# A fused Perceiver layer: the weight product Wq Wk' formed ahead of x, two banks for cross-attention scores, self-attention scores in pairs

## Chip, cores, metric

The kernel is one program on one NeuronCore of a Trainium2 chip. The metric is device time in microseconds (us) of one execution. All numbers here are of the kernel before unless said otherwise.

## What is computed

```python
# x: (4, 128, 512), ctx: (4, 2048, 384), all float32
q, k, v = ln(x) @ Wq + bq, ctx @ Wk + bk, ctx @ Wv + bv
x = x + softmax(q @ k.T / sqrt(512)) @ v             # one head, 2048 keys per batch
cq, ckv = ln(h @ W_dq) * g + b, ln(h @ W_dkv) * g + b # h = ln(x)
K, V = split(ckv @ W_ukv)                            # 16 heads of 32
s = (cq @ W_uq) @ K.T / sqrt(32)                     # zeros and future keys masked
x = x + (softmax(s) @ V) @ W_o.T
# then 16 routed experts (top 4 of 2 groups of 4) and a shared one, relu(x W)^2 W'
```

## The kernel before

**Cross-attention without keys or values.** The scores are q·k = (ln(x) Wq + bq) Wk'·ctx, plus a constant of each query, q·bk. So the kernel forms `qk = Wk q` once for all 512 tokens (`qk_h`, `qk_l`) and multiplies it with the transposed context. Nearly every product is done in three matmuls (`split_mm`): each operand is kept as a rounded part (`_h`, cast by ScalarE) and the rest (`_l`, subtracted by VectorE or GpSimd).

**Setup, before the steps.** SyncE's queue loads x, `wq` (1 MB in one transfer), small vectors, context chunks and `wkT`. VectorE takes moments and normalises four batches (`moments`, `normalise`), PE transposes them (`rows_T`, L1234), ScalarE and VectorE make `xT_h` and `xT_l` (L645, L859). PE forms qT (48 matmuls of 512 columns into banks 4 to 7), ScalarE and VectorE evict it with the bias (L687, L1024), PE forms qk (36 matmuls into banks 4 to 6), it is evicted (L690, L1028), and 32 matmuls of two columns give q·bk (L1262, L1263, `c_mm`), reduced to `ccol`.

**Steps.** After that each engine runs the same loop over steps 1 to 33, and in a step each does its share of several stages in an order written out by hand. There are 16 chunks g of 512 keys, four a batch. In step g+1 PE computes the scores of chunk g into bank 2 (9 matmuls, L1227 to L1229), VectorE evicts them with their maximum (L1078); ScalarE and VectorE split the next chunk into `cT_h`, `cT_l` (L652, L1012), with two buffers of `cT`. Softmax needs the maximum over four chunks, so five steps later (`LAG`) PE transposes the weights (L1360) and multiplies them with the untransposed context (L1436; a float32 matmul is two passes in the trace). Each step after that carries a piece of a batch's remaining work: steps 9, 13, 17 and 21 project with Wv and add the result, steps 12, 16, 20 and 24 make `qk_s` and `v_s` (L1404, L1472).

**Self-attention units.** From step 13 on one unit u enters a step: four heads that sit in rows 32r to 32r+31 of `qk_s`. `unit_scores` (L1334) are four matmuls of contraction 32 into bank 6 or 0, VectorE masks and takes the maximum (L867, L869, L871), ScalarE exponentiates (L759), GpSimd divides (L570), two steps later PE transposes (L1344). Before, most units from 6 on are issued at the end of the step ahead of their own (`early`); a unit waits for the exponentials of unit u-2.

**Queues.** SyncE's queue issues in program order and stops at each wait. The transposed chunks (`load_chunk_T`, four slots) wait until VectorE has split the chunk four before; the others (`load_chunk`, three slots) wait for L1436 of the chunk three before. The first three of these are loaded in setup. `woT` is loaded ahead of transposed chunk 4, behind a wait for the low part of `wv`.

**Later stages** (from about 235 us) are the experts; the change touches there only which semaphore a weight load counts on.

## Time and profile before

| | |
|---|---|
| median of 3 runs | 414.12 us (413.81 to 414.54) |
| the profiled execution's own time | 414.46 us |
| its span | 412.7 us |
| PE busy | 368.5 us |
| DVE (VectorE) busy | 252.6 us |
| ACT (ScalarE) busy | 166.0 us |
| POOL (GpSimd) busy | 97.5 us |

The span runs from the first to the last instruction of the profile; the time is 1.76 us longer. PE's busy time counts pipelined matmuls up to their modelled ends, so starts are safer to read than durations. PEclk is the granted clock of PE in tenths, or as a mean in a window.

### The profile page before, as it was taken

Reading aid. Unit: us, or ns where it says so; the run is one execution under the profiler, and the core shown is the slowest. Engines: PE = TensorE matmul, PEld = TensorE weight load, DVE = VectorE, ACT = ScalarE, POOL = GpSimd, SP = SyncE. Lnnn points to the kernel's source line nnn. Section 1 sums busy time; section 2 is a strip of 40 time slices with the busy share of each in tenths; the row PEclk is TensorE's granted clock in tenths of the full one; section 3 lists DMA queues with packets and bytes.
Section 4 is the critical chain, followed back from the end, with each engine's and each line's share of the span. In section 5 each row is a group of like instructions: output and inputs, shape, how many; then the busy total and the mean of one; then the engine's idle time right before and its main releaser. Section 6 shows DMA issues by size and latency. Waiting matters only on the chain.

```text
span 412.7 us, 5990 instructions
## 1 busy us (share of the span) xinstructions
PE 368.5 (89%) x2116; PEld 254.5 (62%) x2116; DVE 252.6 (61%) x474; ACT 166.0 (40%) x398; POOL 97.5 (24%) x111
## 2 busy tenths in 40 slices
PE   1799869999999998997898799995999999999994
PEld 1578547677677766776677588882544554554452
DVE  5782765565487475477845658933113677776677
ACT  2624455535555564454747606200232332332310
POOL 4740000000011111312413140025334444441200
PEclk9999689999999999999979899996999999999998
DMA  7990396885322254070000460579963433331393
GB/s 246 417 381 5 138 353 261 294 276 197 113 76 78 86 182 169 25 305 2 26 2 28 152 231 22 181 294 360 422 230 122 128 116 116 127 123 59 119 370 124
DMA packets 15998, 71.74 MB, mean 174 GB/s; under 512 B 2913, under 2 KB 2913, under 8 KB 13281
## 3 DMA queue, kind: packets, MB, share of 16 engines
q1 hardware_dynamic: 11808, 57.72, 37.7%
q0 software_dynamic: 4160, 13.63, 9.6%
q8 instruction: 17, 0.28, 0.3%
q14 instruction: 13, 0.10, 0.1%
HBM read 62.96 MB, written 8.39 MB: 173 GB/s over the span
## 4 chain that ended last, share of the span: by engine, by line
PE 64%; DVE 15%; DMA 7%; ACT 4%; issue 4%; POOL 3%; SPq 1%; DVEq 0%; POOLq 0%; ACTq 0%
PE bank L1580 10%; PE bank L1436 9%; PE bank L1554 8%; PE bank L1227 7%; PE bank L1229 6%; PE bank L1228 6%; DMA xs<-x_rows,from_row 4%; DVE cT L1012 4%; PE bank L1334 3%; DVE res L1207 3%; PE bank L1535 2%; DMA raw<-in_wkT 2%; PE bank L1565 2%; PE bank L1404 2%; DMA ring_T<-in_ctxT 2%
## 5 line engine op out<-in xcount | busy, mean ns | idle before, releaser
L1436 PE MATMUL bank<-ring,wT 128*128 128x384 f32 x128 | 43.9, 486 | 0.0
L1012 DVE TENSOR_TENSOR cT<-ring_T,cT 128x512 fp32r<-128x512 f32 x48 | 37.9, 839 | 8.5 <-ACT cT L652 8.4
L1147 DVE COPY xsT<-bank 128x512 f32<-128x512 f32 x24 | 16.6, 690 | 35.1 <-PE bank L1535 25.2
L592 POOL DMA_INDIRECT xs<-x_rows,from_row x24 | 23.3, 969 | 52.1 <-DVE to_row L993 29.8
L547 POOL TENSOR_TENSOR rstd<-var,mhalf 128x1 f32<-128x1 f32 x12 | 6.9, 578 | 111.9 <-DVE var L844 111.9
L1436 PEld LDWEIGHTS bank<-ring,wT 128*128 128x128 f32 x128 | 23.9, 191 | 13.5
L599 POOL DMA_INDIRECT y_rows<-ys,to_row x21 | 22.4, 1067 | 41.2 <-ACT ys L804 41.2
L652 ACT CAST cT<-ring_T 128x512 fp32r<-128x512 f32 x48 | 26.8, 617 | 12.9 <-PE bank L1229 10.3
L1580 PE MATMUL bank<-down_copy,hsT 128*64 128x512 f32 x128 | 31.0, 605 | 0.5 <-DVE ys_l L1188 0.5
L804 ACT ACTIVATE ys<-bank,s_cw 128x512 f32<-128x512 f32 x21 | 14.5, 688 | 41.4 <-PE bank L1580 41.4
L1554 PE MATMUL bank<-up_copy,xsT 128*64 128x256 f32 x256 | 30.3, 379 | 0.0
L1163 DVE COPY up_copy<-WX 128x1024 f32 x32 | 20.7, 691 | 15.1 <-issue 15.1
L791 ACT ACTIVATE hs<-bank 128x256 f32<-128x256 f32 x24 | 9.2, 385 | 49.9 <-PE bank L1554 42.6
L570 POOL TENSOR_TENSOR hw<-hw,hrd 128x512 f32<-128x512 f32 x16 | 18.3, 1149 | 45.2 <-DVE hrd L877 45.2
L1554 PEld LDWEIGHTS bank<-up_copy,xsT 128*64 128x64 f32 x256 | 18.4, 137 | 16.1 <-issue 8.8
L759 ACT ACTIVATE hw<-bank,hnb 128x128 f32<-128x128 f32 x64 | 22.7, 371 | 12.4 <-DVE hnb L871 12.3
L1227 PE MATMUL bank<-cT,qk_h 128*128 128x512 f32 x48 | 21.8, 453 | 3.5 <-DVE sc L1078 3.2
L1172 DVE COPY down_copy<-WX 128x1024 f32 x32 | 21.2, 706 | 5.4 <-PE bank L1580 3.0
L1229 PE MATMUL bank<-cT,qk_l 128*128 128x512 f32 x48 | 20.6, 429 | 0.0
L1228 PE MATMUL bank<-cT,qk_h 128*128 128x512 f32 x48 | 20.5, 427 | 0.0
L1227 PE MATMUL bank<-xT_l,UW 128*128 128x256 f32 (+1 forms) x48 | 17.1, 355 | 3.7 <-DVE xT_l L859 2.5
L1334 PEld LDWEIGHTS bank<-qk_s 32*128 32x128 f32 x128 | 16.2, 194 | 6.1 <-issue 6.1
(282 smaller groups left out, 849.5 us busy)
## 6 DMA issues: line engine op xcount, KB each, us to landing
WX<-in_experts SPq DMA_DIRECT2D x16, 1024.0 KB, 7.4
ring_T<-in_ctxT SPq DMA_DIRECT2D x16, 768.0 KB, 6.4
ring<-in_ctx SPq DMA_DIRECT2D x16, 768.0 KB, 4.4
yr<-y_rows SPq DMA_DIRECT2D x8, 512.0 KB, 7.3
raw<-in_experts SPq DMA_DIRECT2D x3, 1024.0 KB, 5.3
res<-in_x SPq DMA_DIRECT2D x4, 256.0 KB, 3.5
raw<-in_wq SPq DMA_DIRECT2D x1, 1024.0 KB, 6.3
raw<-in_woT SPq DMA_DIRECT2D x1, 1024.0 KB, 4.8
```

Source lines behind the costliest of these rows:

```text
L592: nc.gpsimd.indirect_dma_start(out=xs[:, s % NXS, :], out_offset=None, in_=x_rows, in_offset=bass.IndirectOffsetOnAxis(ap=from_row[:, s:s ...
L599: nc.gpsimd.indirect_dma_start(out=y_rows, out_offset=bass.IndirectOffsetOnAxis(ap=to_row[:, s:s + 1], axis=0), in_=ys[:, s % NYS, :], in_ ...
L652: copy(cT[:, g % 2, 0, t, :], ring_T[:, g % RING_T, t, :]).then_inc(cThi_ok, 1)
L759: e = nc.scalar.activation(hw[:, u % 2, j * P:(j + 1) * P], bank[hs_bank(u)][:, j * P:(j + 1) * P], ACT.Exp, bias=hnb[:, b, i:i + 1], accu ...
L1012: V_.tensor_tensor(cT[:, g % 2, 1, t, :], ring_T[:, g % RING_T, t, :], f32(cT[:, g % 2, 0, t, :]), ALU.subtract).then_inc(cTlo_ok, 1)
L1227: mm(dst, a[0], b[1], start=start, stop=False)
L1228: mm(dst, a[0], b[0], start=False, stop=False)
L1229: return mm(dst, a[1], b[0], start=False, stop=stop)
L1334: last = mm(bank[hs_bank(u)][:, o], qk_s[rows, 0, o], qk_s[rows, 1, o], start=True, stop=True)
L1436: last = mm(bank[B_O][:, 0:TD], wT[:, g % 2, k * P:(k + 1) * P], ring[:, g % RING, k, :], start=(c == 0 and k == 0), stop=(c == NCH - 1 an ...
L1554: last = mm(bank[B_H[g % 2]][q * SLOT:(q + 1) * SLOT, 0:IC * P], xsT[:, g % 2, c * P + q * SLOT:c * P + (q + 1) * SLOT], w, start=c == 0, ...
L1580: last = mm(bank[B_Y[g % 2]][q * SLOT:(q + 1) * SLOT, :], hsT[:, g % 2, m * P + q * SLOT:m * P + (q + 1) * SLOT], w, start=m == 0, stop=m ...
```

## The change

1. **Setup.** The host passes Wq transposed. Since Wk Wq' does not depend on x, PE forms M = Wq Wk' (512 x 384, with two more columns for bk) in four rounds h, one for each quarter of the hidden dimension, as the quarters of x, `wqT` and `wkT` arrive (`queries_to_keys`, 48 matmuls of 386 columns into banks 0 to 3), between the transposes of x. It is evicted as `M2`, and one product of M with xT (36 matmuls of 512 columns) gives qk. The bias bq Wk' is a row of 386 (8 small matmuls), turned into columns (`bias4`) by 4 tiny ones and added at the eviction of qk. The 32 tiny matmuls for the constants of the queries move behind the scores of chunk 0, and only VectorE's eviction of these waits for them. Splitting `wkT` stays on GpSimd, all of `wqT` is on VectorE. Adding bv to `res` moves from GpSimd to VectorE, step 7.
2. **Scores' banks.** Odd chunks go to bank 1, so chunk g waits for the eviction of g-2 instead of g-1, and the last part of `qk_s` waits for the last even chunk only.
3. **Pairs.** At every second step from 13 PE issues the scores of units u and u+1, matmul by matmul in turn, at the start of the step, into banks 6 and 0. They wait for the exponentials of unit u-1. `early` is gone.
4. **Loads.** Quarters as above; no untransposed chunk is loaded in setup: they come one behind each transposed chunk from 6 on; `woT` moves behind transposed chunk 8.

```diff
+        def s_bank(g):
+            return (B_S, 1)[g % 2]
...
-            for b in range(NB):
-                sp.dma_start(res[:, b, :], x[b]).then_inc(x_in[b], 16)
-            sp.dma_start(raw[:, 0, :], wq[:, :, :].rearrange("p c n -> p (c n)")).then_inc(raw_in[0], 16)
+            for h in range(DC):
+                sp.dma_start(res[:, h, :], x[h]).then_inc(x_in[h], 16)
+                sp.dma_start(raw[:, 0, h * D:(h + 1) * D], wqT[:, h, :]).then_inc(wqk_in[h], 16)
+                sp.dma_start(raw[:, 1, h * TD:(h + 1) * TD], wkT[:, h, :]).then_inc(wqk_in[h], 16)
+                if h == 0:
+                    sp.dma_start(bk_s[:], bk).then_inc(bqk_in, 16)
+                    sp.dma_start(bq_s[:], bq).then_inc(bqk_in, 16)
...
-            sp.dma_start(bq_s[:], bq).then_inc(small_in, 16)
-            sp.dma_start(bk_s[:], bk).then_inc(small_in, 16)
+            load_chunk_T(0)
+            load_chunk_T(1)
...
-            load_chunk_T(0)
-            load_item(W_K, wkT, DC * TD)
-            load_chunk_T(1)
-            load_chunk(0)
-            sp.wait_ge(w_lo, LO_Q)
-            sp.wait_ge(w_lo_pool, 1)
+            sp.wait_ge(wq_lo_ok, DC)
             load_item(W_V, wv, TC * D)
             load_chunk_T(2)
-            load_chunk(1)
-            sp.wait_ge(w_lo_pool, 2)
+            sp.wait_ge(wk_lo_ok, DC)
             load_item(W_D, wd, DC * 2 * P)
             load_chunk_T(3)
-            load_chunk(2)
-            sp.wait_ge(q_mm, DC)
+            sp.wait_ge(m_mm, DC)
             sp.dma_start(wu_s[:], wu[:, :, :].rearrange("p c n -> p (c n)")).then_inc(wu_in, 16)
-            sp.wait_ge(w_lo, LO_V)
-            load_item(W_O, woT, DC * D)
             for g in range(RING_T, G + LAG + 1):
                 if g < G:
                     load_chunk_T(g)
-                if RING <= g - LAG - 1 < G:
+                if 0 <= g - LAG - 1 < G:
                     load_chunk(g - LAG - 1)
+                if g == 2 * RING_T:
...
-            pool.wait_ge(xn_ok, NB)
-            pool.wait_ge(small_in, 16 * NSMALL)
-            nc.gpsimd.tensor_tensor(res[:], res[:], bv_s[:].unsqueeze(1).to_broadcast([P, NB, D]), ALU.add).then_inc(bv_ok, 1)
+            for h in range(DC):
+                inverse_root(h)
+                pool.wait_ge(wk_hi, h + 1)
+                nc.gpsimd.tensor_tensor(wk2[:, 1, h, 0:TD], raw[:, 1, h * TD:(h + 1) * TD], f32(wk2[:, 0, h, 0:TD]),
...
-            item_hi(W_Q, wq_h, 2 * HALF)
-            for b in range(NB):
-                rows_hi(b, b, bank[4 + b])
-            item_hi(W_K, wk_h, DC * TD)
+            def query_key_hi(h):
+                act_e.wait_ge(wqk_in[h], 32)
+                copy(wq_h[:, h * D:(h + 1) * D], raw[:, 0, h * D:(h + 1) * D]).then_inc(wq_hi, 1)
+                copy(wk2[:, 0, h, 0:TD], raw[:, 1, h * TD:(h + 1) * TD]).then_inc(wk_hi, 1)
+            query_key_hi(0)
+            for h in range(1, DC):
+                query_key_hi(h)
+                rows_hi(h - 1, h - 1, bank[3 + h])
+            rows_hi(NB - 1, NB - 1, bank[3 + NB])
+            for d in range(DC):
+                act_e.wait_ge(m_mm, d + 1)
+                copy(M2[:, 0, d, :], bank[d][:, 0:TDB]).then_inc(mhi_ok, 1)
...
-            act_e.wait_ge(small_in, 16 * NSMALL)
-            for j in range(DC):
-                act_e.wait_ge(q_mm, j + 1)
-                nc.scalar.activation(qT_h[:, j, :], bank[4 + j][:], ACT.Identity, bias=bq_s[:, j:j + 1]).then_inc(qhi_ok, 1)
+            act_e.wait_ge(row_mm, 1)
+            copy(row_s[:], bank[7][0:2, 0:TDB]).then_inc(row_ok, 1)
+            act_e.wait_ge(bias_ok, 1)
             for t in range(TC):
                 act_e.wait_ge(qk_mm, t + 1)
-                copy(qk_h[:, t, :], bank[4 + t][:]).then_inc(qkhi_ok, 1)
+                nc.scalar.activation(qk_h[:, t, :], bank[4 + t][:], ACT.Identity, bias=bias4[:, t:t + 1]).then_inc(qkhi_ok, 1)
+            act_e.wait_ge(small_in, 16 * NSMALL)
...
-            for b in range(NB):
+            def query_lo(h):
+                dve.wait_ge(wq_hi, h + 1)
+                V_.tensor_tensor(wq_l[:, h * D:(h + 1) * D], raw[:, 0, h * D:(h + 1) * D], f32(wq_h[:, h * D:(h + 1) * D]),
+                                 ALU.subtract).then_inc(wq_lo_ok, 1)
+            def first_moments(b):
                 dve.wait_ge(x_in[b], 16)
                 moments(b, b)
-            for b in range(NB):
...
+            query_lo(0)
+            first_moments(1)
+            normalise(0, 0)
+            query_lo(1)
+            first_moments(2)
+            normalise(1, 1)
+            query_lo(2)
+            first_moments(3)
+            normalise(2, 2)
+            query_lo(3)
+            normalise(3, 3)
             for b in range(NB):
                 rows_lo(b, b, bank[4 + b])
+            for d in range(DC):
+                dve.wait_ge(mhi_ok, d + 1)
+                V_.tensor_tensor(M2[:, 1, d, :], bank[d][:, 0:TDB], f32(M2[:, 0, d, :]), ALU.subtract).then_inc(mlo_ok, 1)
...
+            dve.wait_ge(bias_mm, 1)
+            V_.tensor_copy(bias4[:], bank[3][:, 2 * NB:2 * NB + TC + 1]).then_inc(bias_ok, 1)
+            dve.wait_ge(bias_ok, 1)
...
-            V_.tensor_reduce(out=ccol[:], in_=bank[3][:, 0:2 * NB].rearrange("p (b i) -> p b i", b=NB),
-                             op=ALU.add, axis=AX.X).then_inc(c_ok, 1)
-            dve.wait_ge(c_ok, 1)
+                V_.scalar_tensor_tensor(out=qk_l[:, t, :], in0=bank[4 + t][:], scalar=bias4[:, t:t + 1],
...
+                dve.wait_ge(small_in, 16 * NSMALL)
+                link(V_.tensor_copy(gate_h[:], gate_s[:]))
+                V_.tensor_tensor(gate_l[:], gate_s[:], f32(gate_h[:]), ALU.subtract).then_inc(small_ok, 1)
+                V_.tensor_tensor(res[:], res[:], bv_s[:].unsqueeze(1).to_broadcast([P, NB, D]), ALU.add).then_inc(bv_ok, 1)
...
+                link(V_.tensor_reduce(out=ccol[:], in_=bank[3][:, 0:2 * NB].rearrange("p (b i) -> p b i", b=NB), op=ALU.add, axis=AX.X))
+                V_.tensor_scalar(ccol[:], ccol[:], bias4[:, TC:TC + 1], None, ALU.add).then_inc(c_ok, 1)
...
+                    query_constants()
+                if step == POST - 2:
+                    small_parts()
                 g = step - 1
...
+            def queries_to_keys(h):
+                pe.wait_ge(wq_lo_ok, h + 1)
+                pe.wait_ge(wk_lo_ok, h + 1)
+                if h == 0:
+                    pe.wait_ge(bk_ok, 1)
+                for d in range(DC):
+                    o = h * D + d * P
+                    last = split_mm(bank[d][:, 0:TDB], (wq_h[:, o:o + P], wq_l[:, o:o + P]), (wk2[:, 0, h, :], wk2[:, 1, h, :]),
+                                    h == 0, h == DC - 1)
+                    if h == DC - 1:
+                        last.then_inc(m_mm, 1)
+            for h in range(DC - 1):
+                queries_to_keys(h)
+                rows_T(h, bank[4 + h])
+            rows_T(NB - 1, bank[3 + NB])
+            queries_to_keys(DC - 1)
             pe.wait_ge(xlo_ok, NB)
-            for j in range(DC):
-                for c in range(DC):
-                    o = c * D + j * P
-                    last = split_mm(bank[4 + j][:], (wq_h[:, o:o + P], wq_l[:, o:o + P]), (xT_h[:, c, :], xT_l[:, c, :]),
...
+            for h in range(DC):
+                for i in range(2):
+                    last = mm(bank[7][0:2, 0:TDB], bq2[:, h, :], wk2[:, i, h, :], start=h == 0 and i == 0, stop=h == DC - 1 and i == 1)
+            last.then_inc(row_mm, 1)
             for c in range(DC):
-                pe.wait_ge(qlo_ok, max(c + 1, TC))
+                pe.wait_ge(mlo_ok, c + 1)
...
+                    last = split_mm(bank[4 + t][:], (M2[:, 0, c, t * P:(t + 1) * P], M2[:, 1, c, t * P:(t + 1) * P]),
...
-            pe.wait_ge(small_ok, 2)
-            for b in range(NB):
-                for c in range(DC):
-                    mm(bank[3][:, 2 * b:2 * b + 2], qT_h[:, c, tok(b)], bk2[:, c, :], start=c == 0, stop=False)
-                    last = mm(bank[3][:, 2 * b:2 * b + 2], qT_l[:, c, tok(b)], bk2[:, c, :], start=False, stop=c == DC - 1)
-            last.then_inc(c_mm, 1)
+                if c == 0:
+                    pe.wait_ge(row_ok, 1)
+                    pe.wait_ge(mlo_ok, DC)
+                    for t in range(TC):
+                        mm(bank[3][:, 2 * NB + t:2 * NB + t + 1], row_s[:, t * P:(t + 1) * P], ones[0:2, 0:1], start=True, stop=True)
+                    mm(bank[3][:, 2 * NB + TC:2 * NB + TC + 1], row_s[:, TD:TD + 1].to_broadcast([2, P]), ones[0:2, 0:1],
+                       start=True, stop=True).then_inc(bias_mm, 1)
+            def query_constants():
+                for b in range(NB):
+                    for c in range(DC):
+                        mm(bank[3][:, 2 * b:2 * b + 2], xT_h[:, c, tok(b)], M2[:, :, c, TD], start=c == 0, stop=False)
+                        last = mm(bank[3][:, 2 * b:2 * b + 2], xT_l[:, c, tok(b)], M2[:, :, c, TD], start=False, stop=c == DC - 1)
+                last.then_inc(c_mm, 1)
...
-            def early(u):
-                return u % ROWS != 0 and u >= ROWS + 2
...
+            def pair_scores(u):
                 b, r = divmod(u, ROWS)
-                rows = slice(r * DH, (r + 1) * DH)
                 pe.wait_ge(qkv_ok, 3 * b + 2)
-                before = [v for v in range(u) if hs_bank(v) == hs_bank(u)]
-                if before:
-                    pe.wait_ge(exp_ok, before[-1] + 1)
+                if u >= 2:
+                    pe.wait_ge(exp_ok, u)
                 for j in range(HT):
-                    o = slice(j * P, (j + 1) * P)
-                    last = mm(bank[hs_bank(u)][:, o], qk_s[rows, 0, o], qk_s[rows, 1, o], start=True, stop=True)
-                last.then_inc(hs_mm, 1)
+                    for i in range(2):
+                        rows = slice((r + i) * DH, (r + i + 1) * DH)
+                        o = slice(j * P, (j + 1) * P)
+                        last = mm(bank[hs_bank(u + i)][:, o], qk_s[rows, 0, o], qk_s[rows, 1, o], start=True, stop=True)
+                last.then_inc(hs_mm, 2)
...
+                if (u := unit_at(step, 0)) is not None and u % 2 == 0:
+                    pair_scores(u)
...
-                        pe.wait_ge(c_ok, 1)
                         pe.wait_ge(qklo_ok, TC)
-                    else:
-                        pe.wait_ge(s_ok, g)
+                    elif g >= 2:
+                        pe.wait_ge(s_ok, g - 1)
...
+                        last = split_mm(bank[s_bank(g)][:], (qk_h[:, t, tok(b)], qk_l[:, t, tok(b)]),
...
+                    if g == 0:
+                        query_constants()
...
                         if i == 0 and step <= G:
-                            pe.wait_ge(s_ok, step)
+                            pe.wait_ge(s_ok, step - (step - 1) % 2)
...
-                if (u := unit_at(step, -1)) is not None and early(u):
-                    unit_scores(u)
```

PE, the start of the program, before (rows of `bank<-ident,xn` are transposes of x; `UW` holds wq, `DW` wk):

```order
L1234 MATMUL bank4<-ident,xn 128x128 x4
L1234 MATMUL bank7<-ident,xn 128x128 x4
L1227 MATMUL bank4<-xT_l,UW_61 128x512
L1228 MATMUL bank4<-xT_h,UW_61 128x512
L1229 MATMUL bank4<-xT_h,UW_61 128x512
...
L1228 MATMUL bank7<-xT_h,UW_61 128x512
L1229 MATMUL bank7<-xT_h,UW_61 128x512
L1227 MATMUL bank4<-qT_l_55,DW_62 128x512
L1228 MATMUL bank4<-qT_h_54,DW_62 128x512
```

and of the changed kernel (`UW` is wqT, `wk2` is wkT with bk, `M2` the product, `bq2` the bias):

```order
L1270 MATMUL bank0<-wk2_63,UW_61 128x386
L1271 MATMUL bank0<-wk2_63,UW_61 128x386
L1272 MATMUL bank0<-wk2_63,UW_61 128x386
L1270 MATMUL bank1<-wk2_63,UW_61 128x386
L1277 MATMUL bank4<-ident,xn 128x128 x4
...
L1270 MATMUL bank3<-wk2_63,UW_61 128x386
L1271 MATMUL bank3<-wk2_63,UW_61 128x386
L1272 MATMUL bank3<-wk2_63,UW_61 128x386
L1304 MATMUL bank7<-wk2_63,bq2 2x386 x8
L1270 MATMUL bank4<-xT_l,M2_54 128x512
L1271 MATMUL bank4<-xT_h,M2_54 128x512
```

The transposes stood ahead of everything; now the first 12 matmuls of the weight product do, and x is needed by 36 matmuls of 512 columns instead of 84.

SyncE's queue from the first context chunk on, before (`ring_T` are transposed chunks, `ring` the others):

```order
L430 DMA ring_T<-in_ctxT 128x1536
L433 DMA raw<-in_wkT 128x1536
L430 DMA ring_T<-in_ctxT 128x1536
L425 DMA ring<-in_ctx 128x1536
L433 DMA raw<-in_wv 128x1536
L430 DMA ring_T<-in_ctxT 128x1536
L425 DMA ring<-in_ctx 128x1536
L433 DMA raw<-in_wd 128x1024
L430 DMA ring_T<-in_ctxT 128x1536
L425 DMA ring<-in_ctx 128x1536
L456 DMA wu_s<-in_wu 128x1536
L433 DMA raw<-in_woT 128x2048
```

and in the changed kernel from `wv` on:

```order
L448 DMA raw<-in_wv 128x1536
L445 DMA ring_T<-in_ctxT 128x1536
L448 DMA raw<-in_wd 128x1024
L445 DMA ring_T<-in_ctxT 128x1536
L464 DMA wu_s<-in_wu 128x1536
L445 DMA ring_T<-in_ctxT 128x1536 x3
L440 DMA ring<-in_ctx 128x1536
L445 DMA ring_T<-in_ctxT 128x1536
L440 DMA ring<-in_ctx 128x1536
L445 DMA ring_T<-in_ctxT 128x1536
L440 DMA ring<-in_ctx 128x1536
L448 DMA raw<-in_woT 128x2048
```

Three `ring` loads have left the setup and `woT` stands behind the third `ring` load.

PE in steps 16 to 19, before (`qk_s` rows are the self-attention scores; x4 in the program is 8 passes in the trace; L1360 opens a step):

```order
L1472 MATMUL bank<-wu_s,cf 128x512
L1334 MATMUL bank<-qk_s 128x128 x4
L1360 MATMUL bank<-ident,sc 128x128 x4
...
L1229 MATMUL bank<-wv_w,DW 128x512
L1334 MATMUL bank<-qk_s 128x128 x4
L1360 MATMUL bank<-ident,sc 128x128 x4
L1334 MATMUL bank<-qk_s 128x128 x4
L1344 MATMUL bank<-ident,hw 128x128 x4
```

and in the changed kernel, same steps:

```order
L1530 MATMUL bank<-wu_s,cf 128x512
L1393 MATMUL bank<-qk_s 128x128 x8
L1419 MATMUL bank<-ident,sc 128x128 x4
...
L1272 MATMUL bank<-wv_w,DW 128x512
L1419 MATMUL bank<-ident,sc 128x128 x4
L1403 MATMUL bank<-ident,hw 128x128 x4
...
L1277 MATMUL bank<-ident,xn 128x128 x4
L1393 MATMUL bank<-qk_s 128x128 x8
L1419 MATMUL bank<-ident,sc 128x128 x4
```

Three blocks of four became two blocks of eight; the second now stands behind the transposes of `xn` at the end of step 18.

## Rows read from the trace of the kernel before

**Rows 1.** Page, the chain that ended last, by engine.

```profile
PE 64%; DVE 15%; DMA 7%; ACT 4%; issue 4%; POOL 3%; SPq 1%; DVEq 0%; POOLq 0%; ACTq 0%
```

**Rows 2.** Windows by stage: busy time of each engine, PEclk, DMA.

```profile
core 0: us, PE busy (x) PEld busy (x) DVE busy (x) ACT busy (x) POOL busy (x), PEclk, DMA share, GB/s
14.60:27.50 12.90, 12.85 (x48) 10.01 (x48) 10.79 (x8) 5.10 (x7) 8.53 (x2) 1.00 1.02 419
27.50:40.70 13.20, 11.91 (x69) 10.41 (x68) 3.80 (x8) 5.38 (x8) 0.00 (x0) 1.00 0.23 85
40.70:58.00 17.30, 12.01 (x37) 8.27 (x38) 13.43 (x24) 6.86 (x13) 0.00 (x0) 0.80 0.60 238
58.00:80.00 22.00, 22.00 (x85) 15.60 (x86) 10.77 (x22) 12.04 (x26) 0.00 (x0) 0.92 0.73 265
110.00:182.50 72.50, 69.65 (x398) 52.00 (x397) 45.66 (x98) 41.32 (x127) 11.46 (x14) 1.00 0.35 125
182.50:235.00 52.50, 43.60 (x339) 35.88 (x339) 34.06 (x64) 30.55 (x97) 14.18 (x15) 0.90 0.17 63
```

**Rows 3.** Timeline, PE in setup: start, us, line, operation.

```profile
27.12 0.40 PE L1229 MATMUL bank<-xT_h,UW 128*128 128x512 f32 x1
...
36.57 0.39 PE L1229 MATMUL bank<-qT_h,DW 128*128 128x512 f32 x1
...
40.18 0.25 PE L1263 MATMUL bank<-bk,qT_l 128*128 128x2 f32 x1
40.73 0.47 PE L1227 MATMUL bank<-cT,qk_h 128*128 128x512 f32 x1 [0.31 <-issue]
```

**Rows 4.** The chain in order of time, one matmul at each pace.

```profile
36.51 0.23 PE bank L1228
...
42.03 0.43 PE bank L1228
```

**Rows 5.** Timeline, the other engines in setup.

```profile
3.51 0.69 DVE L842 BATCH_NORM_STATS2 stats<-res 128x6 f32<-128x512 f32 x1 [3.51 <-DMA res<-in_x]
8.95 1.90 ACT L634 CAST UW<-raw 128x2048 fp32r<-128x2048 f32 x1 [6.87 <-DMA raw<-in_wq]
9.58 0.55 DVE L854 TENSOR_SCALAR xn<-res,mv,rstd 128x512 f32<-128x512 f32 x1 [0.82 <-PE bank L1234]
12.03 2.48 DVE L859 TENSOR_TENSOR xT_l<-bank,xT_h 128x512 fp32r<-128x512 f32 x4
16.73 3.50 POOL L554 TENSOR_TENSOR DW<-raw,DW 128x1536 fp32r<-128x1536 f32 x1 [2.40 <-ACT DW L634]
36.26 2.05 DVE L1028 TENSOR_TENSOR qk_l<-bank,qk_h 128x512 fp32r<-128x512 f32 x3 [7.21 <-ACT qk_h L690]
```

**Rows 6.** DMA issues, 0 to 70 us: KB each, median us to landing.

```profile
bk_s<-in_bk SPq DMA_DIRECT2D x1, 2.0 KB, 5.5
```

**Rows 7.** Timeline, steps 1 to 5: the waits.

```profile
44.88 1.75 DVE L830 TENSOR_TENSOR wv_w<-raw,wv_w 128x1536 fp32r<-128x1536 f32 x1
49.91 0.47 PE L1227 MATMUL bank<-cT,qk_h 128*128 128x512 f32 x1 [0.94 <-DVE sc L1078]
53.34 1.66 ACT L652 CAST cT<-ring_T 128x512 fp32r<-128x512 f32 x3 [2.62 <-DMA ring_T<-in_ctxT]
57.94 0.66 PE L1360 MATMUL bank<-ident,sc 128*128 128x128 f32 x4 [2.08 <-ACT sc L694]
```

**Rows 8.** Timeline, PE, small-array matmuls: one row group, then column groups.

```profile
151.84 1.15 PE L1334 MATMUL bank<-qk_s 32*128 32x128 f32 x8
...
157.76 0.30 PE L1452 MATMUL bank<-hwT_first,v_s 128*32 128x128 f32 x1
...
157.78 0.30 PE L1452 MATMUL bank<-hwT_odd,v_s 128*32 128x128 f32 x1
```

**Rows 9.** Timeline, PE and ACT in the unit steps.

```profile
105.06 1.16 PE L1404 MATMUL bank<-cf,wu_s 128*128 128x128 f32 x8 [0.62 <-DVE sc L1078]
...
157.56 0.37 ACT L759 ACTIVATE hw<-bank,hnb 128x128 f32<-128x128 f32 x1
...
188.11 0.66 PE L1344 MATMUL bank<-ident,hw 128*128 128x128 f32 x4 [1.14 <-POOL hw L570]
```

103 lines of the change are left out of this document (44 added, 59 removed).

## The prediction

> **What bounds the kernel now.** I read the chain first: 64% of the span is PE [rows 1]. The windows by stage say where that is true. PE is fully busy from 58 to 80 us and has 69.65 of 72.50 us in the unit steps up to 182.5, so there every microsecond taken off PE counts. From 182.5 to 235 it has 43.6 of 52.5: other engines' chains end last. Before 58 there are three other stages [rows 2]. PE forms qT until 27.1, qk until 36.6, the 32 tiny matmuls until 40.2, and the first scores begin at 40.73 [rows 3]; DMA is full in the first of these (419 GB/s) and nearly idle in the second. From 40.73 to 57.94 a step waits by turns for VectorE's eviction (0.94 us), a transposed chunk (2.62 us) and the first exponentials (2.08 us) [rows 7].
>
> **Setup, step by step.** Unit costs: 512 columns start every 0.23 us at the high clock and every 0.43 us at half of it [rows 4]. By columns, 386 take 0.175 and 0.325 us (estimates). Other engines: moments about 1.0 us a batch (0.69 us and two small operations), normalising 0.55, a 512-column low part 2.48/4 = 0.62, ScalarE's cast of a quarter of wqT 1.90/4 = 0.48, GpSimd's quarter of wkT 3.50/4 = 0.88 [rows 5].
>
> Round 0 needs x, wqT and wkT quarters. x lands at 3.51 [rows 5]; a round is 256 + 256 + 192 KB, 1.7 us at 419 GB/s [rows 2], so round 0 is in at about 5. Cast, low parts and the bk columns put PE's first matmul near 6.9. From there PE has 12 matmuls at half clock (3.9), 36 at full clock (6.3) and four batches of transposes (about 0.5 each): it ends M near 19. VectorE has 4 x 1.0 moments, 4 x 0.62 wqT, 4 x 0.55 normalising, 4 x 0.62 xT, 4 x 0.5 M and about 1.4 for the biases and their wait, 14.6 us from 3.5: 18. So the two engines are close and PE is last. Then 8 row matmuls (1.4), 36 x 0.23 (8.3), the columns of the bias (0.8): 29.5. Before, the last low part of qk ended at 38.31, 1.35 us after the last matmul's end [rows 3, 5]; the same puts the first scores at 30.8 in place of 40.73: **9.9 us earlier**. What makes this is not only 12 fewer matmul-widths: 48 matmuls now run under loads and normalisation where PE did 16 transposes, and the 32 tiny matmuls (36.6 to 40.2, 3.6 us) leave the front.
>
> Bounds. If PE were at full clock from its first matmul, it would end M at 17, VectorE would set the time with 18, and the scores would start at about 28.3 (12.4 us earlier). If bq and bk take the 5.5 us to land that bk took before [rows 6], VectorE stands behind them in order until about 8.2 and everything is 2.5 us later; if PE stays at half clock through M, 36 x 0.15 = 5.4 us are added. Both: 2.0 us earlier; either alone, 4.5 to 7.4. I take 9.9, since bk stood behind 2 MB before and now behind 0.7 MB, and since PE reached the higher clock during qT.
>
> **Steps 1 to 5.** The 3.6 us of tiny matmuls come back here, behind chunk 0's scores. VectorE's eviction of chunk 0 waits for them, and in its order the low parts of chunk 2 stand behind that eviction. Against it, the 0.94 us waits for an eviction go with the second bank, and the 2.62 us for transposed chunk 4 goes, since `woT` and three untransposed chunks no longer stand ahead of it [rows 7]. Walking VectorE through: 1.9 us of low parts and 0.8 of eviction a step, 1.75 for wv in step 1, 1.2 for wd in step 2; eviction 0 at about 6.7 us after the first scores start, 1 at 9.2 to 10, 2 at 13, 3 at 16.5, and exponentials 2 us on: 18.0 to 18.9 against 17.2 now. I take a **loss of 1.2**; bounds: a gain of 2.6 (VectorE never waits) and a loss of 3.6 (all tiny matmuls on the path). Shift at step 5: 8.7.
>
> **Steps 5 to 12.** PE has no gap in 58 to 80, so a bank more gives nothing there. The 128x2048 add of bv costs VectorE 4 x 0.62 to 4 x 0.7, under 3 us, in step 7, beside about 3 us of its own in a step of 5.1: VectorE is busy 10.77 of 22.0 us [rows 2], and it catches up in step 8. Uncovered it would be 0.5 to 1 us once. GpSimd loses 5 us of work nobody waited for. The loads: a step now moves 2 x 768 KB = 1.57 MB in 5.1 us, 308 GB/s against 419 seen. The second bank removes one visible wait, 0.62 us before `qk_s` at 105.06 [rows 9]: **0.6**.
>
> **Pairs.** A unit's 8 passes take 1.08 us (1.15 to the modelled end), all in one row group. The only matmuls in small arrays that overlap are in column groups: four of 128 columns start within 0.02 us [rows 8]. Row groups into different banks show nowhere. The cost of a pair is then between 1.08 (full overlap) and 2.16 (none); I take 1.2, because rows 8 are the nearest, the same array split the other way. Units 0 to 9 lie in the PE-bound part: 10 x 1.08 become 5 x 1.2, 4.8 less. The pair's start now waits for the exponentials of unit u-1. Those of unit 5 end at about 158.0 [rows 9], while PE, relieved of two blocks, would be there near 157.3: 0.6 lost. For units 2, 4, 8 exponentials end within 0.1 us of PE's arrival or earlier. Units 10 to 15 fall where PE already waits (1.14 us for GpSimd at 188.11 [rows 9]): their six blocks give nothing, with 1 us either way; unit 12's scores come up to 1.2 us later, behind unit 11's exponentials. **4.2 in all** (bounds -1.6, which is serial pairs plus their waits, and 6).
>
> The Trainium skill (TensorE: Matmul & The Clock Gate, Part 3) states that weight loads overlap running matmuls only when the row group differs, and that four row tiles of contraction 32 gave 3.07 times the rate. That supports overlap; taken as 77% efficiency, an estimate from that page makes a pair 1.4 us, and the sum 1.0 us smaller than mine. No row here shows row groups side by side; rows 8 show only the column case.
>
> **Sum.** 9.9 - 1.2 + 0.6 + 4.2 = 13.5 us. Everything behind 235 us starts on events that shift along, the expert loads too. From the profiled execution's 414.46 that gives 401.0; against the median 414.12, **400.6 us**. The two stand 0.08% apart.
>
> **Rivals.**
> - *Row groups don't overlap.* For it: a pass of 128 columns takes 0.135 us, about its weight load, so loads may be what is paced. Then pairs cost 1.6 instead of saving 4.2: sum 7.7, about 406 us. Chance 13%.
> - *Setup stays cold or waits for the bias.* For it: PE needed its first matmuls of qT to leave half clock, and M comes in four bursts with waits between; against it: bursts leave little gap. It costs 2.5 to 6: 403.5 to 407 us. 15%.
> - *Setup is VectorE's and the late pairs help.* Scores at 28.3 and the six late blocks give 1 or 2: 395.5 to 397.5 us. 12%.
> - *Slower: untransposed chunks arrive late.* Chunk 0's load is issued when chunk 2 is split, and L1436 wants it three steps later. Place: `ring` in steps 5 to 16. If the stream rate fell below what a step needs, PE would wait each step; 11 steps must lose 13.5 us, 1.2 each, which is from 1.57 MB/6.3 us = 248 GB/s down. At 230 it would be 417 us. Against it: 419 GB/s in rows 2. 2%.
> - *No change.* The gain reaches 235 us and is given back later, at the gathers that wait for expert weights, if those loads came at a time of their own. They hang on semaphores of the same steps, so 3%: about 414 us.
>
> **How the numbers follow.** The likeliest case has 55%, 397.5 to 403.5 us. The range 395.5 to 407 takes in the first three rivals but the edges and leaves out 15%. A measurement of this kernel can tell about 0.2% (0.8 us) from no change: faster 0.95, same 0.02, slower 0.03.
>
> **What would show it.** Right: first scores (first matmul from `cT`) at 29 to 32 us; from there to the first L1419 transposes 17.5 to 19 us; no DMA releaser ahead of `cT` casts or the product with `ring`; blocks of the pair with 16 passes in about 1.2 us, starts of neighbouring row groups within 0.02 us; PE's wait for the exponentials under 1 us a pair; 182.5 to 235 about as long as before. Wrong: scores after 34 us, PE at half clock in M, VectorE waiting for bq; a pair of 2 us; a transfer as releaser in steps 5 to 12; or a longer tail behind the routing.

## Result and profile after

The changed kernel takes 398.9 us (median; 398.22 to 401.28), the kernel before 414.33 on the same chip (413.81 to 417.3): ratio 0.9605, 95% interval 0.9561 to 0.9648. A second measurement (e9 below) gave 0.9641 (0.9607 to 0.9675). The profiled executions are 414.46 and 398.89 us, 15.6 us apart; the ledger below is theirs.

The page's part on the chain that ended last, by engine, changed kernel (compare [rows 1]):

```profile
PE 63%; DVE 17%; ACT 6%; DMA 5%; issue 4%; POOL 4%; DVEq 0%; SPq 0%; POOLq 0%; ACTq 0%
```

Windows by stage of the changed kernel (compare [rows 2]): loads and first splits, M, the product with x, steps 1 to 5, cross-attention steps, unit steps, late steps.

```profile
core 0: us, PE busy (x) PEld busy (x) DVE busy (x) ACT busy (x) POOL busy (x), PEclk, DMA share, GB/s
0.00:8.10 8.10, 0.00 (x0) 0.03 (x1) 2.97 (x10) 2.31 (x3) 4.24 (x19) 1.00 0.67 176
8.10:21.50 13.40, 13.20 (x65) 12.50 (x66) 9.33 (x21) 6.61 (x13) 5.39 (x6) 1.00 0.86 318
21.50:34.20 12.70, 10.99 (x53) 8.15 (x51) 5.62 (x12) 5.43 (x12) 0.00 (x0) 1.00 0.69 280
34.20:51.60 17.40, 14.03 (x69) 11.17 (x69) 13.59 (x26) 8.76 (x16) 0.00 (x0) 0.90 0.53 195
51.60:73.60 22.00, 21.34 (x92) 15.11 (x92) 14.53 (x29) 13.62 (x28) 0.00 (x0) 1.00 0.98 395
93.00:167.00 74.00, 70.17 (x430) 51.92 (x428) 47.86 (x104) 44.82 (x131) 10.99 (x13) 1.00 0.35 124
167.00:219.20 52.20, 40.23 (x349) 34.36 (x348) 35.73 (x68) 31.35 (x99) 14.67 (x15) 0.90 0.18 70
```

TensorE is still the engine that sets the pace, and nearly always busy in the cross-attention steps (21.3 of 22.0 us). The first window is empty for it. The PEclk of 1.00 in the second window is no measurement up to 13.3 us: the clock's record begins there, and until then the passes start 0.32 us apart, as at half clock; behind it, 0.175.

Timeline of the changed kernel's setup, the rows at which something ends last (compare [rows 3, 5]); the last number in brackets is the idle time ahead and its releaser:

```profile
5.46 0.62 ACT L684 CAST UW<-raw 128x512 fp32r<-128x512 f32 x1 [3.38 <-DMA raw<-in_wkT]
6.57 1.27 POOL L561 TENSOR_TENSOR wk<-raw,wk 128x384 fp32r<-128x384 f32 x1 [1.24 <-ACT wk L685]
8.10 0.66 PE L1270 MATMUL bank<-wk,UW 128*128 128x386 f32 x1 [8.10 <-POOL wk L561]
8.56 0.53 PE L1271 MATMUL bank<-wk,UW 128*128 128x386 f32 x1
8.88 0.53 PE L1272 MATMUL bank<-wk,UW 128*128 128x386 f32 x1
...
21.37 1.56 PE L1304 MATMUL bank<-wk,bq 128*2 128x386 f32 x8
...
32.00 2.07 DVE L1058 SCALAR_TENSOR_TENSOR qk_l<-bank,bias,qk_h 128x512 fp32r<-128x512 f32 x3 [5.80 <-ACT qk_h L702]
...
34.22 0.47 PE L1270 MATMUL bank<-cT,qk_h 128*128 128x512 f32 x1 [1.73 <-DVE qk_l L1058]
```

The first scores start at 34.22 us, 6.5 earlier than before. The passes have the predicted paces, 0.32 us in round 0 and 0.175 later. Steps 1 to 5 and two pairs (compare [rows 7, 8]):

```profile
40.01 0.17 DVE L1070 TENSOR_REDUCE ccol<-bank 128x4 f32<-128x8 f32 x1 [2.08 <-PE bank L1325]
...
40.48 0.75 DVE L1123 TENSOR_SCALAR_CACHE_REDUCE sc<-bank,ccol 128x512 f32<-128x512 f32 x1
...
47.15 0.50 PE L1270 MATMUL bank<-cT,qk_h 128*128 128x512 f32 x1 [1.28 <-DVE cT L1048]
...
51.57 0.66 PE L1419 MATMUL bank<-ident,sc 128*128 128x128 f32 x4 [2.08 <-ACT sc L708]
...
100.78 1.16 PE L1393 MATMUL bank<-qk_s 32*128 32x128 f32 x16
...
174.99 1.16 PE L1393 MATMUL bank<-qk_s 32*128 32x128 f32 x16 [1.57 <-ACT hw L773]
```

Where the 15.6 us come from, by the same block of work in both traces:

| up to | before | after | earlier by | this stage |
|---|---|---|---|---|
| first scores | 40.73 | 34.22 | 6.5 | 6.5 |
| first product with an untransposed chunk | 62.0 | 54.1 | 7.9 | 1.4 |
| eighth such product | 106.0 | 97.2 | 8.8 | 0.9 |
| sixteenth | 173.5 | 159.9 | 13.6 | 4.8 |
| last output projection (`wo_w`) | 234.6 | 218.8 | 15.8 | 2.2 |
| end | 412.7 | 397.2 | 15.5 | -0.3 |

### The profile page after: what moved, and what is told of

Read it like the earlier page. It is cut to its first block, busy times and chain, and to the rows that moved or that the text cites. A ratio compares the mean times of both kernels' runs of the same rounds, so it can differ in the third digit from the quotient of the medians.

```text
span 397.2 us, 6027 instructions
## 1 busy us (share of the span) xinstructions
PE 354.0 (89%) x2132; PEld 246.2 (62%) x2132; DVE 249.3 (63%) x482; ACT 166.6 (42%) x405; POOL 89.7 (23%) x112
## 4 chain that ended last, share of the span: by engine, by line
PE 63%; DVE 17%; ACT 6%; DMA 5%; issue 4%; POOL 4%; DVEq 0%; SPq 0%; POOLq 0%; ACTq 0%
PE bank L1637 10%; PE bank L1611 9%; PE bank L1270 8%; PE bank L1494 7%; PE bank L1272 7%; PE bank L1271 7%; DMA xs<-x_rows,from_row 4%; DVE res L1250 3%; PE bank L1593 2%; ACT hw L773 2%; PE bank L1622 2%; PE bank L1393 1%; PE bank L1464 1%; PE bank L1419 1%; DVE bank L883 1%
## 5 line engine op out<-in xcount | busy, mean ns | idle before, releaser
L596 POOL DMA_INDIRECT xs<-x_rows,from_row x24 | 23.3, 970 | 52.5 <-DVE to_row L1007 29.8
L1048 DVE TENSOR_TENSOR cT<-ring_T,cT 128x512 fp32r<-128x512 f32 x48 | 30.5, 685 | 5.8 <-ACT cT L656 5.8
L773 ACT ACTIVATE hw<-bank,hnb 128x128 f32<-128x128 f32 x64 | 22.7, 371 | 13.2 <-DVE hnb L885 13.1
L1215 DVE COPY down_copy<-WX 128x1024 f32 x32 | 21.5, 714 | 5.8 <-PE bank L1637 3.4
L1270 PE MATMUL bank<-cT,qk_h 128*128 128x512 f32 x48 | 20.9, 436 | 3.0 <-DVE qk_l L1058 1.7
L1272 PE MATMUL bank<-cT,qk_l 128*128 128x512 f32 x48 | 19.5, 405 | 0.0
L1271 PE MATMUL bank<-cT,qk_h 128*128 128x512 f32 x48 | 19.4, 404 | 0.0
L1611 PE MATMUL bank<-WX,xsT 128*64 128x256 f32 x128 | 17.1, 413 | 2.4 <-DVE xsT L1190 2.4
L1593 PE MATMUL bank<-ident,xs 128*128 128x128 f32 x96 | 15.5, 286 | 3.8 <-DMA xs<-x_rows,from_row 3.8
## 6 DMA issues: line engine op xcount, KB each, us to landing
raw<-in_woT SPq DMA_DIRECT2D x1, 1024.0 KB, 11.1
```

Source lines behind the costliest of these rows:

```text
L596: nc.gpsimd.indirect_dma_start(out=xs[:, s % NXS, :], out_offset=None, in_=x_rows, in_offset=bass.IndirectOffsetOnAxis(ap=from_row[:, s:s ...
L773: e = nc.scalar.activation(hw[:, u % 2, j * P:(j + 1) * P], bank[hs_bank(u)][:, j * P:(j + 1) * P], ACT.Exp, bias=hnb[:, b, i:i + 1], accu ...
L1048: V_.tensor_tensor(cT[:, g % 2, 1, t, :], ring_T[:, g % RING_T, t, :], f32(cT[:, g % 2, 0, t, :]), ALU.subtract).then_inc(cTlo_ok, 1)
L1270: mm(dst, a[0], b[1], start=start, stop=False)
L1271: mm(dst, a[0], b[0], start=False, stop=False)
L1272: return mm(dst, a[1], b[0], start=False, stop=stop)
```

## Experiments

Each kernel was timed against the kernel before on the same chip; ratios carry 95% intervals. Block times are from one profiled execution each. "The product" is the first product with an untransposed chunk, which ends the stage of steps 1 to 5; the first and the sixteenth such product, and the last output projection, mark the stages as in the table above.

Part of each kernel's scatter goes with TensorE's clock, of which every timed execution lists its mean. So executions at like clocks are compared as well (a single figure is one execution; where in it the clock fell is not listed):

| kernel | mean clock | us |
|---|---|---|
| before | 0.964 to 0.966 | 413.6 to 415.4 |
| changed (two measurements) | 0.972, 0.973 | 398.2 to 398.9 |
| changed | 0.964, 0.965 | 398.9 to 400.0 |
| e4, six units singly | 0.973 | 400.8 |
| e5, one bank | 0.965 | 402.9 |
| e6, unit by unit | 0.972 | 401.9 |
| e7, constants split | 0.973 | 396.7 and 397.4 |
| e8, second queue | 0.972, 0.973 | 399.9 to 400.6 |
| e12, old load order | 0.973 | 398.0 and 398.5 |

**e1, setup and loads alone.**

```diff
-            return (B_S, 1)[g % 2]
+            return B_S
+                if (u := unit_at(step, 0)) is not None and not early(u):
+                    unit_scores(u)
```

> The changed setup and load order alone: the chunks' scores use one bank again and the self-attention scores are formed unit by unit as before. Theory A (the parts add up as the block-by-block comparison of the two traces says): first scores at 34.2 us, the first product with an untransposed chunk 7.9 us earlier than before, and 7.9 us less at the end: 406.4 us. Theory B (the second bank is what lets chunks 0 to 4 pass without loss, so the setup alone gives back part of its gain there): scores at 34.2 us, but steps 1 to 5 take about 18.4 in place of 17.4 us: 407.5 us. Theory C (the late phase's extra 2.2 us comes from the setup and the loads, not from the pairs): 404.2 us.

Ratio 0.9872 (0.9843 to 0.9901), 410.61 us; profiled 411.48, 3.0 below the profile before. The scores start at 33.2, but the first product with an untransposed chunk only at 58.6: of 7.5 us, 3.4 are left. Theory B named the stage (25.4 us from scores to product, before 21.3) and undersized it; A and C fell. The lines on `s_ok`, by which PE waits for the eviction of g-1 again, go with the two shown.

**e2, pairs alone.** Before with `pair_scores` in place of `unit_scores`.

> The kernel before with the self-attention scores in pairs of units and nothing else. Theory A (a pair of 16 passes takes 1.16 us and the pairs give 4.8 us in the stage where TensorE never rests and 2.2 us behind it): 407.4 us. Theory B (the pairs give only the 4.8 us; the late 2.2 us has another source): 409.6 us. Theory C (TensorE's time is freed but the exponentials, the eviction chain or the transposed chunks take it back, since nothing else of the change is there): 412 us or more.

Ratio 0.988 (0.9848 to 0.9913), 410.13 us. Sixteenth product 4.7 us earlier, last output projection 3.8, end 4.2: theory B. Its clock was low in the late stage (below).

**e3, bank alone.** Before with `s_bank` and its waits.

> The kernel before with a second bank for the chunks' scores and nothing else. Theory A (the bank removes the 0.94 us waits for evictions in steps 2 to 4 only to run into the wait for transposed chunk 4, which stays, and saves 0.9 us near 105 us): 413.5 us. Theory B (the waits of steps 2 to 4 are worth their sum too): 412 us. Theory C (nothing waits for the eviction once TensorE is the bound): 414.3 us.

Ratio 0.9958 (0.9929 to 0.9987), 414.56 us: 1.7 us, between 0.5 and 2.9. In the profile scores to first product take 21.5 us as before (21.3), from there to the eighth product 0.9 less, and the end comes 0.8 earlier: theory A. By itself the bank gives nothing in steps 1 to 5.

**e4, pairs up to unit 9 only.** Units 10 to 15 with `unit_scores`, early as before.

> The changed kernel with pairs for units 0 to 9 only; units 10 to 15 are formed one by one, early where the kernel before formed them early. Theory A (the late phase's extra 2.2 us comes from the pairs of units 10 to 15): 401.1 us, with the last output projection of the attention 2.2 us later than in the changed kernel. Theory B (it comes from the setup's side, or from bias and loads having left GpSimd and the queues): 398.9 us.

Ratio 0.9687 (0.9651 to 0.9723), 402.18 us. Up to the sixteenth product as the changed kernel (14.0 us earlier than before), then 62.8 us to the last output projection against 58.9 (before 61.1). Theory A, though 3.5 us are lost where it said 2.2. The interval is clear of that of the first measurement and overlaps e9's.

**e5, changed kernel with one bank.** The first two lines of e1's diff and the waits on `s_ok`; pairs stay.

> The changed kernel with the chunks' scores in one bank again, pairs and setup as changed. Theory A (bank and setup work together: with the constants' 32 small matmuls behind chunk 0 and one bank, TensorE stands between the first chunks and stays at half clock until about 50 us as in the run of the setup alone): the first product with an untransposed chunk starts at 58 to 59 us instead of 54.1, half clock costs 5 us or more between 38 and 60 us instead of 1.7, and the time is 403 to 404 us. Theory B (the long half clock in the run of the setup alone was that execution's own; the bank is worth its visible waits only): product at 55 us, time 399.5 to 400.5 us.

Ratio 0.9771 (0.9723 to 0.9819), 407.47 us. Product at 58.6, then 5.3 us late behind it: theory A by its stage; the time is 3.5 us above its 403 to 404. Timeline of TensorE in e5:

```profile
41.40 0.76 PE L1270 MATMUL bank<-cT,qk_h 128*128 128x512 f32 x1 [1.41 <-DVE sc L1123]
...
46.52 0.77 PE L1270 MATMUL bank<-cT,qk_h 128*128 128x512 f32 x1 [0.94 <-DVE sc L1123]
```

Windows from the first scores to that product: before, the changed kernel, e5, e1, e12, e3 (columns as above).

```profile
40.70:62.00 21.30, 16.01 (x49) 11.53 (x50) 15.33 (x27) 9.49 (x18) 0.00 (x0) 0.76 0.62 239
```
```profile
34.20:54.10 19.90, 16.53 (x81) 13.34 (x82) 15.48 (x29) 11.26 (x21) 0.00 (x0) 0.91 0.59 221
```
```profile
34.20:58.60 24.40, 19.02 (x81) 14.76 (x82) 15.64 (x29) 11.28 (x21) 0.00 (x0) 0.79 0.59 211
```
```profile
33.20:58.60 25.40, 19.99 (x81) 15.62 (x82) 15.68 (x29) 11.44 (x21) 0.00 (x0) 0.75 0.61 215
```
```profile
32.90:55.50 22.60, 19.62 (x81) 16.02 (x82) 15.52 (x29) 11.45 (x21) 0.00 (x0) 0.77 0.62 225
```
```profile
41.80:63.30 21.50, 14.62 (x49) 10.97 (x50) 15.11 (x27) 9.39 (x18) 0.00 (x0) 0.84 0.61 236
```

Each span has three parts. Waits are the span less TensorE's busy time. What half clock added is half of the time that TensorE was busy inside its stretches at 1.2 GHz (before: 5.9 us from 41.6 to 48.4 and 3.3 behind 58.7, so 4.6). The rest is the work at full clock. It is an estimate, since busy time uses modelled ends:

| | span | waits | half clock | work |
|---|---|---|---|---|
| before | 21.3 | 5.3 | 4.6 | 11.4 |
| e3, bank alone | 21.5 | 6.9 | 3.2 | 11.4 |
| changed | 19.9 | 3.4 | 1.7 | 14.9 |
| e5, one bank | 24.4 | 5.4 | 4.2 | 14.9 |
| e1, one bank, no pairs | 25.4 | 5.4 | 5.3 | 14.8 |
| e12, e6, e11, two banks | 22.6 to 22.7 | 2.9 to 3.0 | 5.1 | 14.6 |
| e7, constants split | 17.9 | 3.2 | 1.6 | 13.0 |

The 32 small matmuls cost the stage their 3.4 us of work in every form of the new setup, and e7, with 16 of them moved out, 1.6. The second bank takes out 2.0 us of waits (e5 against changed). Half clock is the rest, and it is not the bank's alone: two-bank kernels with the same matmuls in this stage lost 1.7 us (both profiles of the changed kernel, e4, e8) or 5.1 (e6, e11, e12). e5 compares well with the changed kernel, since up to 39.8 us TensorE did the same in both and the clock fell at nearly the same time (40.7 and 40.6 us); after that e5's TensorE waited for the evictions above and had 1.2 GHz until 51 us, the changed kernel's went on without a wait and was back at 2.4 GHz at 44.0. At like clocks of whole executions (0.965, one of them e5's) the second bank is worth 3 to 4 us on top of the new setup; by e5's ratio against those of the changed kernel's two measurements it is 5 to 7.

**e6, the eight passes of one unit, then the eight of the other.**

```diff
-                for j in range(HT):
-                    for i in range(2):
+                for i in range(2):
+                    for j in range(HT):
```

> The changed kernel with the 16 passes of a pair in another order: the eight of the first unit, then the eight of the second, instead of by turns. Theory A (a pass overlaps only the pass next to it, in the other row group): a block takes 2.1 to 2.2 us in place of 1.16, the 16th product starts 5 us later and the time is 405 us. Theory B (the 1.16 us come from something else, such as twice the work under one wait): blocks near 1.2 us and 399 us.

Ratio 0.9739 (0.9687 to 0.9792), 407.0 us. One pair in e6:

```profile
102.40 1.71 PE L1393 MATMUL bank<-qk_s 32*128 32x128 f32 x16
```

1.71 us is between the theories: even so the passes overlap in part (a unit by itself took 1.15 [rows 8]). By turns, two passes start 0.007 us apart and the next two 0.11 us later; unit by unit, three couples among the 16 still start within 0.007 us. The four pairs ahead of the sixteenth product lose 1.3 us together against the changed kernel, not the 5 of theory A. What makes the pair cheap is the overlap of row groups, and the order by turns makes it whole. Of the rest of e6's loss 1.6 us lie before the first unit, in code that is the same (below).

**e7, constants split.** 16 small matmuls ahead of the first scores, 16 behind chunk 1's. The column of M that they read is copied first, since the chunks' evictions overwrite it.

```diff
+            V_.tensor_copy(m_col[:], M2[:, :, :, TD]).then_inc(col_ok, 1)
...
                    if g == 0:
+                        query_constants(0)
                         pe.wait_ge(qklo_ok, TC)
...
+                    if g == 1:
+                        query_constants(1)
```

> The changed kernel with the 32 small matmuls of the query constants split: 16 of them (batches 0 and 1) in TensorE's gap before the first scores, 16 behind chunk 1's scores. Theory A (VectorE's eviction of chunk 0 at 40.5 us, behind all 32, holds up the low parts of chunks 2 and 3): the eviction moves to about 37, TensorE's 1.28 us wait for a low part at 47 and part of its 2.08 us at 51.6 go, product with the first untransposed chunk 1.5 to 3 us earlier, time 396 to 397.4 us. Theory B (transposed chunks arrive too late to use it, or the exponentials end last all the same): product within 0.5 us, 398.9 us.

Ratio 0.9555 (0.952 to 0.959), 397.88 us: the fastest of all by its ratio. VectorE's timeline in e7:

```profile
37.86 0.23 DVE L1076 TENSOR_SCALAR ccol<-ccol,bias 128x2 f32<-128x2 f32 x1
38.12 0.75 DVE L1130 TENSOR_SCALAR_CACHE_REDUCE sc<-bank,ccol 128x512 f32<-128x512 f32 x1
```

The eviction starts 2.4 us earlier than in the changed kernel (not 3.5), the product at 51.8, 2.3 earlier: theory A. In the profiled execution the late steps gave 2.0 of it back, with 17.1 us of them at half clock instead of 10.2. The interval lies clear of e9's, not of the first measurement's.

**e8, wkT on ScalarE's queue.**

```diff
-                sp.dma_start(raw[:, 1, h * TD:(h + 1) * TD], wkT[:, h, :]).then_inc(wqk_in[h], 16)
+                nc.scalar.dma_start(raw[:, 1, h * TD:(h + 1) * TD], wkT[:, h, :]).then_inc(wqk_in[h], 16)
```

> The changed kernel with the four quarters of wkT issued by ScalarE at its start instead of by SyncE between the others. Theory A (the 14 issues of 0.43 to 0.73 us each, until 8.0 us, are what spreads the first weights): the last quarter of wkT lands by 8 us, ScalarE no longer waits until 9.53 us for the second, TensorE ends M 1 to 2 us earlier and the first scores start at 32.2 to 33.3 us; 396.9 to 398 us. Theory B (the packets of 1.5 and 2 KB are what holds the rate at 180 to 255 GB/s): landing and scores as before within 0.3 us, 398.9 us. Theory C (ScalarE's issues delay its own casts): first scores later than 34.2 us.

Ratio 0.9646 (0.9596 to 0.9696), 401.28 us. Windows from 4 to 8 us, the changed kernel and e8, and two rows of e8's timeline:

```profile
4.00:8.00 4.00, 0.00 (x0) 0.00 (x0) 2.44 (x10) 1.03 (x2) 1.85 (x2) 1.00 0.81 219
```
```profile
4.00:8.00 4.00, 0.00 (x0) 0.00 (x0) 1.53 (x5) 1.03 (x2) 1.03 (x2) 1.00 0.94 285
```
```profile
6.44 0.62 ACT L683 CAST UW<-raw 128x512 fp32r<-128x512 f32 x1 [2.47 <-DMA raw<-in_wqT]
7.50 0.17 DVE L1026 CAST bq<-bq_s 128x4 fp32r<-128x4 f32 x1 [1.93 <-DMA bq_s<-in_bq]
```

The rate rose from 219 to 285 GB/s, so one queue does hold it down; whether by the time of its issues isn't separated. But all quarters now share it: the first pieces and bq land later, the first matmul starts at 9.5 instead of 8.1, the scores at 35.0. No theory had both halves; C's outcome came by another road. At like clocks it is 1 to 2 us slower than the changed kernel.

**e9, the changed kernel again.**

> The changed kernel once more, for a second profiled execution. Theory A (the late phase, from the 16th product with an untransposed chunk to the last output projection, took 58.9 us in the first profile because TensorE spent little of it at half clock; the other kernels with pairs took 60.9 to 64.2 us there): the blocks up to 173 us within 0.3 us of the first profile unless the clock falls before 60 us, the late phase 59 to 62 us, and the difference equal to the difference in time lost at half clock; 399 to 401 us. Theory B (the 2.2 us that the late phase gave are the pairs' and steady): late phase 58.9 us within 0.3, 398.9 us.

Ratio 0.9641 (0.9607 to 0.9675), 399.93 us. All blocks within 0.3 us of the first profile, the late phase 59.0 us. Theory B, though A allows it too, since the half clock was that of the first profile.

**e10, split constants, and ScalarE casts wkT before wqT.**

> The version with the split constants, and in the setup ScalarE casts each quarter of wkT before that of wqT, since TensorE's first matmul waited for GpSimd's low part of wkT. Theory A (that chain starts M): first matmul at 7.5 to 7.7 us instead of 8.10, first scores 0.4 to 0.6 us earlier than in the version with split constants alone (34.0), the first product with an untransposed chunk at 51.3 us, 397 us. Theory B (VectorE's low part of wqT, now later, ends last instead): first matmul within 0.2 us of 8.10 and no change behind it; 397.5 us.

Ratio 0.9597 (0.9558 to 0.9635), 399.2 us. First matmul at 7.64, behind another releaser, and scores at 33.6, 0.3 before e7's. Rows of e10:

```profile
5.84 1.00 POOL L563 TENSOR_TENSOR wk<-raw,wk 128x384 fp32r<-128x384 f32 x1 [0.46 <-ACT wk L686]
5.89 0.97 DVE L1029 TENSOR_TENSOR bq<-bq_s,bq 128x4 fp32r<-128x4 f32 x1
...
7.64 0.66 PE L1277 MATMUL bank<-wk,UW 128*128 128x386 f32 x1 [7.64 <-DVE UW L1017]
```

A's half of it holds and B's too: VectorE is last now. The product comes at 53.0, 1.2 later than in e7, with half clock from 49.5 us. It isn't shown that this version is better than e7; their intervals overlap.

**e11, the addition of bv on GpSimd.**

> The changed kernel with the addition of bv to x given back to GpSimd, as soon as its inputs are there (about 20 us), so that it runs beside VectorE's low parts of M and of chunk 0. Theory A (VectorE and GpSimd hold each other up: in the profile before, VectorE's first low parts of a transposed chunk took over 9 us beside GpSimd's work and 1.9 us in the changed kernel): VectorE's low parts of M or of the chunk take more than 1 us each while GpSimd adds, the product of M with x starts up to 3 us later or the first scores do, 400 to 403 us. Theory B (GpSimd's work is independent): VectorE's means within 10%, first scores at 34.2 us, 398.9 us.

Ratio 0.9691 (0.9654 to 0.9728), 403.22 us. GpSimd's add and VectorE's low parts of chunk 0 beside it in e11:

```profile
18.54 4.66 POOL L565 TENSOR_TENSOR res<-res,bv_s 128x2048 f32<-128x2048 f32 x1 [1.18 <-DMA gb_s<-in_gammas_betas]
```
```profile
21.82 3.13 DVE L1051 TENSOR_TENSOR cT<-ring_T,cT 128x512 fp32r<-128x512 f32 x3
```

The low parts took 3.13 us in place of 1.88 and nobody waited: scores at 33.1. The low parts of xT and M, which read a bank, kept their 2.47 and 1.94 us beside the same add. So A's effect is there and off the path. The time fell in A's range, but not by A's road: waits in steps 1 to 5 are 3.0 us (changed 3.4), and the later product (55.9) comes with 5.1 us at half clock, as in e6 and e12. The interval overlaps e9's.

**e12, load order of before.**

> The changed kernel with the load order of before behind the setup: untransposed chunks 0 to 2 between the transposed ones, and woT ahead of transposed chunk 4. Theory A (these 3 MB ahead of transposed chunk 4 are what made step 4 wait 2.62 us before): ScalarE's cast of chunk 4 waits 1.5 to 3.5 us for its transfer, the first product with an untransposed chunk starts at 56 to 57.5 us instead of 54.1, and the time is 401 to 402.5 us. Theory B (the queue had 195 GB/s of its 420 in use from 34 to 52 us, so the 3 MB fit in): product within 0.5 us of 54.1, 398.9 us.

Ratio 0.9648 (0.9603 to 0.9692), 401.6 us. No cast waits for a transposed chunk. Product at 55.5 with the clock of 0.77 above, as e6 (55.8, also 0.77) which has the new order: theory B by its cause, though the product is outside its 0.5 us. At the highest clock the two load orders take the same time (398.0 and 398.5 here, 398.2 to 398.9 in the changed kernel). SyncE's waits from 10 to 60 us, before and e12:

```profile
SPq L433 <- DVE wv_w L830: 18.8, 1, 18.8
```
```profile
SPq L448 <- DVE wv_w L846: 16.1, 1, 16.1
```

woT is issued behind the low part of wv: at 46.7 us before, at 36.7 in e12, and transposed chunk 4 stands behind it in both. The change put that low part ahead of the constants and of chunk 0's eviction in VectorE's order (36.2 instead of 44.9 [rows 7]). That, with the whole stage, is the likely reason why chunk 4 came in time; moving it alone wasn't tried.

## Why the prediction held, and where its steps were off

The forecast (400.6, range 395.5 to 407) held for both measurements. Its sum of 13.5 us against 15.6 has errors of both signs: the setup gave 3.4 us less than forecast, steps 1 to 5 gave 2.6 more, the bank 0.3, the units 0.6, the late stage 2.2. That they cancel down to 2.1 us is luck, and part of the gain is clock that no term foresaw.

- **Setup, 9.9 forecast, 6.5 measured.** The unit costs were right (0.32 and 0.175 us a pass of 386 columns). The first matmul came at 8.10, not 6.9 (1.2): round 0 was in at 5.46 instead of 5, and behind it stood two casts and a low part of 1.27 us instead of 0.88. M then took 13.3 us instead of 12.1 (1.2): its 48 passes 10.8 instead of 10.2, and the transposes between the rounds, with a wait of 0.2 for GpSimd's low part at 16.0, 2.5 instead of 2.0. Row, product and bias took 10.9 instead of 10.5 (0.4), the last eviction 1.9 instead of 1.35 (0.55). The step "1.7 us at 419 GB/s" failed outright, for the same queue moved 176 GB/s in the first 8.1 us, but it accounts for 0.5 of the 3.4; the rest is the chain of casts and low parts behind it and a number of small terms put too low. This is the rival "setup stays cold or waits for the bias" in size and only in part by its causes: bq held VectorE for 1.20 us until 5.87 and the first matmul still waited for GpSimd; half clock in round 0 was as forecast and lasted into the second round, to 13.3 us. My own mark of "wrong", scores after 34 us, was met.
- **Steps 1 to 5, a loss of 1.2 forecast, 0.1 to the transposes at 51.57 and a gain of 1.4 to the product.** By the table of parts, work grew by the 3.4 us of the small matmuls, near the 3.6 forecast; waits fell by 1.9; and half clock, for which the sum had no term, fell by 2.9. Without the last the loss would have been 1.5. Transposed chunk 4 went as forecast, but not for the reason forecast (e12).
- **Bank, 0.6 forecast.** In the profiles 0.8 alone (e3) and 5.3 on top of the new setup (e5 against the changed kernel): 0.9 at 105 us, 4.5 in steps 1 to 5, of which 2.0 are waits and 2.5 half clock. It was priced on the kernel before, where the small matmuls did not stand between chunks 0 and 1.
- **Pairs, 1.2 us each: 1.16.** The total came out (4.2 net for units 0 to 9 forecast), its working did not. Only four pairs, units 0 to 7, stand ahead of the sixteenth product, and they gave 4.8: a pair saved 1.2 us and not 0.96, because a unit's block holds TensorE longer than its eight passes. From the last matmul before it to the first behind it, the eight single blocks took 1.3 to 2.0 us each (12.0 in all), the four pairs 1.6 to 2.0 (7.2). Units 8 and 9 gave 1.0 more in the late stage. The wait at unit 6 was 0.26 us instead of 0.6, and 0.26 and 0.20 came at units 2 and 8. The rival "row groups don't overlap" is gone. The estimate of 1.4 us from the Trainium skill (TensorE: Matmul & The Clock Gate, Part 3) was too dear here. Its rule that loads overlap only when the row group differs agrees in direction with 1.71 us (by units) against 1.16 (by turns), both for 16 passes; it doesn't explain why one change of row group leaves as little as 1.71.
- **Late units (10 to 15), 0 with 1 us either way: about 1.2 of the stage's 2.2.** That they "fall where PE already waits" was half right. Windows from the sixteenth product to the last output projection: before, the changed kernel, e4, e2, e7.

```profile
173.50:234.60 61.10, 52.23 (x382) 41.91 (x381) 38.09 (x72) 35.81 (x113) 14.66 (x15) 0.92 0.23 86
```
```profile
159.90:218.80 58.90, 45.92 (x383) 37.86 (x381) 38.06 (x72) 36.01 (x114) 14.67 (x15) 0.91 0.21 81
```
```profile
159.50:222.30 62.80, 52.91 (x382) 42.42 (x381) 38.41 (x72) 35.74 (x113) 14.66 (x15) 0.89 0.23 84
```
```profile
168.70:230.80 62.10, 51.49 (x382) 42.24 (x381) 39.09 (x72) 36.03 (x113) 14.66 (x15) 0.84 0.22 83
```
```profile
157.60:218.50 60.90, 50.45 (x382) 41.76 (x381) 38.96 (x72) 36.09 (x114) 14.68 (x15) 0.86 0.20 79
```

In three parts as above: work 47.3 us before and 46.3 in e4, 42.2, 41.9 and 42.0 with all pairs; waits 8.9, 9.9 and then 13.0, 10.6, 10.5; half clock 4.9, 6.7 and then 3.8, 9.6, 8.5. So the pairs of units 10 to 15 free about 4 us of TensorE's work here (e4 against the changed kernel), as the prediction did not expect, and part comes back as waits (1.6 us for the exponentials at each of the pairs from units 10 and 12) and, in e2 and e7, at half clock. Why the clock stayed high in the changed kernel's two profiles and less in e2's and e7's is open: the blocks are the same, their times shifted by 2 to 9 us. In e2 nothing of it reached the end of the stage. At a clock of 0.973 e4 takes 400.8 us, 1.9 to 2.6 above the changed kernel.

- **bv, loads, tail: nothing.** The tail gave back 0.3.
- **A rival's price.** The prediction puts a stream of 230 GB/s at 417 us. By its own figures it is about 420: 1.57 MB take 6.8 us a step instead of 5.1, 11 times. Nothing of it came: no product and no cast of steps 5 to 12 waited for a transfer.
- **Signs.** Met: blocks of a pair of 1.16 us with neighbours' starts 0.007 us apart, no DMA releaser, a late stage as long as before (52.2 against 52.5 us in the last rows of the windows by stage). Missed: the scores at 34.2 instead of 29 to 32, 17.4 us to the transposes where 17.5 to 19 were given, and waits for exponentials of 1.57 and 1.58 us where under 1 was given.

## What to carry to other kernels

Price a wait on the kernel as it will be after the other parts of the change: the bank was worth 0.8 us alone and 5.3 together with the setup in the profiles, 3 to 4 of them at like clocks. Before reading a gain or a loss, split the stage into waits, half clock and work; span times clock mixes them, since the work of other engines does not slow with TensorE's clock (VectorE's low parts of a chunk took 1.88 us at full and 1.89 at half clock). Compare timed executions at like clocks too: the same kernel moved by 4 to 6 us with its mean clock (e11, e12). Price a small block by the time from its neighbour to its neighbour and not by its own passes (1.3 to 2.0 us against 1.08 here). In this kernel, work that a stage is freed of was best put into an existing gap of the same engine (e7), not behind the first thing that others wait for.

## What was not expected of the hardware

- **VectorE held by GpSimd.** The kernel before, VectorE's first two low parts of chunk 0 in narrow windows, and GpSimd's add:

```profile
17.21 3.57 DVE L1012 TENSOR_TENSOR cT<-ring_T,cT 128x512 fp32r<-128x512 f32 x1 [2.06 <-ACT cT L652]
```
```profile
20.70 5.11 DVE L1012 TENSOR_TENSOR cT<-ring_T,cT 128x512 fp32r<-128x512 f32 x1
```
```profile
20.19 5.07 POOL L558 TENSOR_TENSOR res<-res,bv_s 128x2048 f32<-128x2048 f32 x1
```

Each takes 0.68 us alone. The first ended at 20.78, 0.55 after GpSimd's low part of wkT [rows 5], the second at 25.81, 0.55 after the add. In e10 a subtraction of 128x4 took 0.97 us, to the end of GpSimd's operation at 6.84. Operations that read a bank were not held (e11). The Trainium skill (GPSIMD Engine Reference, Specifications) states that GpSimd contends with VectorE instructions that have two SBUF inputs; the traces agree, with a hold until GpSimd's whole operation ends. The prediction hadn't drawn on it.
- **The same start, another clock.** TensorE reached the full pace of M at 13.3 us in the changed kernel's profile and at 11.1 in e6, in code that is the same. e6's scores start 1.0 us earlier (33.2), its clock then falls from 38.4 us on for 6.8 us instead of 3.4 and once more at 52, and its first product is 1.6 us later. A setup faster by 1 us was no gain there. e11 and e12 (full pace at 10.9 and 10.8, scores at 33.1 and 32.9) lost the same 5.1 us in steps 1 to 5; the changed kernel again, e4 and e8 (13.1, 12.2, 13.3) lost 1.7. What sets these times is not shown.
- **One queue.** 14 issues of 0.38 to 0.73 us each last until 8 us, at 176 GB/s; a second queue brought 30% more rate and a later first piece (e8).
